# Four-layer selective-scan network on one Trainium2 core: the input products of both channel halves as one VectorE operation between two scans

## What is computed

```python
xs    = four orders of the convolved activation      # [B, 4, 256, 4096]
dts, Bs, Cs = split(einsum('bkdl,kcd->bkcl', xs, x_proj_w), [8, 24])
delta = softplus(einsum('bkrl,kdr->bkdl', dts, dt_w) + dt_b)
A     = -exp(A_log)                                  # [4, 256, 16]
def step(h, t):
    h = exp(d_t[..., None] * A) * h + (d_t * x_t)[..., None] * B_t[:, :, None, :]
    return h, einsum('bkdn,bkn->bkd', h, C_t)
```

## Time and profile before

| | |
|---|---|
| median of three runs | 26486.41 us |
| lowest and highest run | 26484.9 and 26491.68 us |
| span of the profiled execution, first to last instruction | 26472.5 us |
| time of the profiled execution beyond its span | not recorded; the median of the runs is 13.9 us above the span |
| DVE busy | 25249.3 us (95%), 28655 instructions |
| PE busy | 20800.8 us (79%) |
| POOL busy | 16821.7 us (64%) |
| ACT busy | 16551.4 us (63%) |
| mean granted TensorE clock | 0.957 of 2.4 GHz |

### The profile page before, as it was taken

The page is one execution under the profiler, slowest core; times in us unless marked ns, Lnnn a source line. Parts: engine busy times, 40 slices in busy tenths (PEclk is TensorE's granted clock), DMA queues, the critical chain, the costliest instruction groups (busy, mean ns, idle before and its releaser), DMA issues.

```text
span 26472.5 us, 271753 instructions
## 1 busy us (share of the span) xinstructions
PE 20800.8 (79%) x48516; PEld 8224.1 (31%) x49344; DVE 25249.3 (95%) x28655; ACT 16551.4 (63%) x31677; POOL 16821.7 (64%) x7108
## 2 busy tenths in 40 slices
PE   7778778778777777877877877787778778778777
PEld 3333333333333333333333333333333333333333
DVE  9998998998999899899899899969999998998998
ACT  6665665665666566666566566656666665665665
POOL 5765765775677477577577567707775765775775
PEclk9999999999999999999999999999999999999999
DMA  0000000000000000000000000010000000000000
GB/s 15 7 0 17 7 0 16 0 7 16 1 7 4 16 7 1 16 0 7 16 0 7 10 7 7 0 58 1 7 4 13 7 0 16 0 7 16 1 7 7
DMA packets 53095, 222.41 MB, mean 8 GB/s; under 512 B 4384, under 2 KB 4512, under 8 KB 45600
## 3 DMA queue, kind: packets, MB, share of 16 engines
q1 hardware_dynamic: 51744, 209.22, 2.1%
HBM read 125.31 MB, written 83.89 MB: 8 GB/s over the span
## 4 chain that ended last, share of the span: by engine, by line
issue 48%; DVE 34%; PE 7%; ACT 7%; DVEq 3%; POOL 0%; DMA 0%; ACTq 0%; another core or an unknown queue 0%; POOLq 0%; SPq 0%
DVE WK L584 21%; DVE WK L567 7%; PE PS L361 3%; DVE WK L561 2%; ACT PS L787 2%; DVE WK L558 2%; PE PS L474 1%; PE PS L487 1%; ACT YP L771 1%; DVEq L577 1%; DVEq L579 1%; DVE X L645 1%; ACT CS L780 1%; ACT WK L762 1%; PE PS L349 1%
## 5 line engine op out<-in xcount | busy, mean ns | idle before, releaser
L937 POOL TENSOR_TENSOR HC<-WK,CS 128x1024 f32<-128x1024 f32 x6144 | 14824.7, 2415 | 7065.8 <-DVE WK L584 5702.7
L584 DVE TENSOR_TENSOR_SCAN WK<-PS,CARRY,WK 128x512 f32<-128x512 f32 x12288 | 15593.2, 1269 | 114.0 <-ACT PS L787 99.5
L787 ACT ACTIVATE PS<-WK,ANEG 128x512 f32<-128x512 f32 x12288 | 8452.0, 691 | 8013.6 <-DVE WK L584 8009.6
L361 PE MATMUL PS<-HC,KC 128*128 128x512 f32 x24576 | 12368.4, 628 | 648.9 <-ACT YP L771 641.3
L567 DVE TENSOR_TENSOR WK<-WK,PS 128x512 f32<-128x512 f32 x12288 | 8055.4, 656 | 46.6 <-DVE WK L584 45.0
L349 PE MATMUL PS<-PARTS,SEL 128*128 128x512 bf16 x11616 | 3727.7, 398 | 4715.8 <-DVE WK L567 4560.8
L361 PEld LDWEIGHTS PS<-HC,KC 128*128 128x128 f32 x24576 | 4849.4, 200 | 5367.6 <-issue 3879.4
L349 PEld LDWEIGHTS PS<-PARTS,SEL 128*128 128x128 bf16 x12288 | 1155.0, 99 | 9761.2 <-DVE WK L567 8332.6
L780 ACT ACTIVATE CS<-PS 128x512 f32<-128x512 f32 x6144 | 3586.9, 584 | 379.2 <-PE PS L349 358.4
L924 POOL TENSOR_TENSOR WK<-WK 128x1024 f32<-128x1024 f32 x384 | 911.4, 2373 | 2416.4 <-DVE WK L555 2416.4
L767 ACT ACTIVATE CARRY<-WK 128x2 f32<-128x2 f32 x5376 | 1012.8, 188 | 0.0
(11 more groups left out here) (114 smaller groups left out, 11580.2 us busy)
## 6 DMA issues: line engine op xcount, KB each, us to landing
gates<-WK SPq DMA_DIRECT2D x96, 512.0 KB, 3.0
X<-gates SPq DMA_DIRECT2D x12, 4096.0 KB, 12.8
X<-hidden SPq DMA_DIRECT2D x20, 2048.0 KB, 8.0
hidden<-WK SPq DMA_DIRECT2D x96, 256.0 KB, 2.0
X<-in_x SPq DMA_DIRECT2D x8, 2048.0 KB, 8.8
YP<-hidden SPq DMA_DIRECT2D x4, 2048.0 KB, 9.2
out<-WK SPq DMA_DIRECT2D x32, 256.0 KB, 2.0
W<-w SPq DMA_DIRECT2D x3, 2004.5 KB, 12.4
```

The source lines that it names most:

```text
L361: mm = pe.matmul(YB[:, h], ident, HC[:, slot, h], start=(n == 0), stop=(n == N - 1))
L584: dve.tensor_tensor_scan(c.run(HS[n % RING][:, h]), c.run(DAB[:, h]), c.run(DBX[n % 2][:, h]), CARRY[:, n, h:h + 1], ALU.mult, ALU.add).th ...
L787: act.activation(DAB[:, h], DELTA[par][:, h], ACT.Exp, scale=ANEG[:, a:a + 1])\
L937: pool.tensor_tensor(HC[:, n % RING], HS[n % RING], both(CS[:, n % RING]), ALU.mult).then_inc(s["readout_ready"], 1)
```

## The change

Each step's two input products of 128 x 512 become one of 128 x 1024, in which the B row in PSUM is read once for each half through `both`. It is issued between scan (n, half 0) and scan (n, half 1), so that scan (n, half 1) and scan (n+1, half 0) follow each other directly. `input_ready` counts one per step and no longer two, and its readers wait for the new counts. No other engine's work is changed.

```diff
@@ pe, chunk
                     if n + 2 < N or nxt:
-                        pe.wait_ge(s["input_ready"], st * DH + DH)
+                        pe.wait_ge(s["input_ready"], st + 1)
@@ dve
-            def scan_input(st, slot, par, h):
-
-                if h == 0:
-                    dve.wait_ge(s["b_ready"], st + 1)
-                dve.tensor_tensor(DBX[slot][:, h], DX[par][:, h], BB[:, slot], ALU.mult).then_inc(s["input_ready"], 1)
+            def scan_input(st, slot, par):
+
+                dve.wait_ge(s["b_ready"], st + 1)
+                dve.tensor_tensor(DBX[slot], DX[par], both(BB[:, slot]), ALU.mult).then_inc(s["input_ready"], 1)

             def chunk(c, prev, nxt, par):
                 for n in range(N):
                     st = c.step + n
                     for h in range(DH):
-                        if n + 1 < N or nxt:
-                            if n + 1 == N and h == 0:
+                        if h == 1 and (n + 1 < N or nxt):
+                            if n + 1 == N:
                                 dve.wait_ge(s["dx_ready"], nxt.i + 1)
                             if prev or n >= 1:
-                                dve.wait_ge(s["state_ready"], st * DH + (h - 1))
-                            scan_input(st + 1, (n + 1) % 2, par if n + 1 < N else 1 - par, h)
-                        dve.wait_ge(s["input_ready"], st * DH + (h + 1))
+                                dve.wait_ge(s["state_ready"], st * DH)
+                            scan_input(st + 1, (n + 1) % 2, par if n + 1 < N else 1 - par)
+                        if h == 0:
+                            dve.wait_ge(s["input_ready"], st + 1)
@@ dve, ahead of an image's first chunk
-                        for h in range(DH):
-                            scan_input(first.step, 0, 0, h)
+                        scan_input(first.step, 0, 0)
```

## The result

The changed kernel takes 26640.12 us, median of four runs (26633.9 to 26643.44), against 26485.9, the median of four, for the kernel before: a ratio of 1.0058, with a 95% interval of 1.0044 to 1.0072. It is slower by 0.6%, where 0.8% faster was forecast, and lies outside the range. The spans differ by 26638.3 - 26472.5 = 165.8 us.

What follows compares the result with a forecast made beforehand. The prediction took DVE, busy 95% of the span, to bound the kernel. Its terms, -400 + 50 + 112 + 32 = -206 us on 26486, gave 26280 us, with a range of 26095 to 26510.

Steps and rivals of the forecast that it cites:

- The step: DVE's scan-to-scan, scan-to-product and product-to-scan starts: 1.195 + 1.17 + 1.12 = 3.485 us a step, against 3.55 before.
- -400 us: DVE's saving over 6144 steps, at 0.065 us less per step.
- Rival C: On DVE, two products share a real fixed part of 0.12 us, which merging saves: 25943 us; chance 0.07.
- The waits on exp0: Scans on DVE stall for ACT's exp0 in steps 5, 6 and 13, adding 50 + 112 + 32 us.
- Step 13: In direction 0, behind ACT's turned copy, exp0 comes late for the scan: 96 chunks x 0.52 = 50 us.
- steps 5 and 6: Scans wait for exp0 in chunks taking an odd or even chunk's sums: 112 and 32 us.
- where odd sums are taken: In 180 chunks, exp0 comes late in steps 5 and 6 behind ACT's long copy: +112 us.
- even ones: In step 6 of 192 chunks taking an even chunk's sums, 101 have too little exp0 margin: +32 us.
- Everywhere else exp0 keeps enough: Outside steps 5, 6 and 13 no new stall; least margin 1.09 us in step 8, 0.3 above what stalls.
- stays: POOL starts on the half 1 scan, whose place between same-half neighbours is unchanged; no cost was given.
- Rival D: Slower: PE drops to 1.2 GHz in even chunks too, lengthening stalls in steps 4 to 6: 26696 us; chance 0.08.
- the chain of steps 4 to 6: PE's sums after `y_merged`, leading to exp0 and the scan: 1.8 us a chunk at TensorE's 1.2 GHz.

Runs made afterwards that it cites:

- e4: The changed kernel with its one 1024-column product written as two of 512 columns at the same place between the scans; 27044.64 us.
- e3: The kernel before, with the operations L555 and L561 moved behind the scan of half 1 of steps 8 and 14; 26163.66 us, ratio 0.988.

## Why the prediction was wrong

- **The step.** Forecast 3.485 us from 1.195 + 1.17 + 1.12, measured 3.481, with 1.11 from product to scan. This part of the mechanism held. The -400 us are there, and e4 shows that they are the merging. Rival C's fixed part of 0.12 us does not exist in the distance between starts: e4 prices one operation saved in each step at 405 / 6144 = 0.066 us. The Trainium skill, *Perfetto Trace Analysis*, section "Optimizing Scalar/DVE Operations", gives a DVE operation on PSUM a fixed access cost of about 125 ns. The summed durations are near it (657 + 674 ns in e4 less 1191 here are 140 ns). The distance between starts is not, and the kernel's time follows the distance.
- **The waits on exp0.** Forecast +194 us in steps 5, 6 and 13, measured +184 us. Step 13 gave 44 for 50, steps 5 and 6 together 141 for 144. The two kinds of chunks agree as well, 104 us where odd sums are taken (112 forecast) and 30 where even ones are (32), so this is no sum of errors that cancel. In idle time it is 245.5 us in 482 waits, for some 270 in 500.
- **The step that failed.** "Everywhere else exp0 keeps enough", and with it the sum's silence on L555 and L561. The prediction asked of each operation on DVE whether it waits for ACT, and of POOL only that its own start "stays". It did not ask what DVE does while POOL runs. Its two rows on ordinary steps hold only operations that read PSUM, for which POOL does not matter. The missing term is 384 x (0.577 + 0.578) = +444 us.
- **It could have been read before.** L555 took 1275 ns in the scan, L561 1574, though L558, with the same size and two operands in SBUF, took 1190. An operation of DVE that lasts far longer than its like, with no idle time before it, hides a wait. And L555's end lay 0.54 us behind the readout's in the trace quoted above.
- **Rival D**, slower by the chain of steps 4 to 6, had the sign but not the cause: that chain cost what the forecast said.
- **Smaller.** Step 0 brought 67 us that no step of the prediction had; 45 of it are the pauses of the earlier trace rows ahead of a product at the loop's turn. What the pauses come from was not tried. That a scan now comes first there is not enough to explain it: step 0 is longer than an undisturbed step by 68 us in all in the kernel before, by only 30 in e3, where a product still comes first, and by 27 in e4, where a scan does (16 of them put down to ACT's copy of the last column).

The terms as they should have stood: -400 + 184 + 444 - 67 = +161 us.

## What to carry to other kernels

Before moving an operation on DVE, list which of the operations that move with it have all tensor operands in SBUF, and see in the timeline whether POOL is at work when they start: they end when POOL is done, and every bit of time by which they start earlier is lost. Put such operations right behind the event that releases POOL, so that DVE is there first, and let POOL, which has room, wait. See what stands behind them in their new place: in e3 a product had to wait for the end of L561. A duration well above that of the same form elsewhere in the trace is a wait that the profile does not call idle, and the price of an instruction in a full stream is the distance of starts, not the duration.

## What the runs showed of the hardware

- DVE's TENSOR_SCALAR of 128 x 1024 in f32, SBUF to SBUF, took 666 ns with POOL quiet, and ended 0.54 to 0.56 us after a POOL operation that was in flight when it started, whether its own start was 0.75 or 1.33 us ahead of that end (kernels before and after). A TENSOR_TENSOR of 128 x 1024 with both operands in SBUF took 1197 ns with POOL quiet and ended 1.08 to 1.09 us after. The other way round, a POOL operation that started 0.16 us behind them took 2.72 us (TENSOR_SCALAR) and 3.26 us (TENSOR_TENSOR) for 2.36.
- A tensor_tensor_scan that follows a scan lasts 1.25 us instead of 1.27 and hands over 0.02 us earlier; in the changed kernel, where every scan of half 0 follows one, the means are 1255 ns for half 0 and 1270 for half 1.
- Merging two 512-column products on one PSUM operand into one of 1024 saved 0.066 us between starts, 0.14 in summed durations (e4).
